# Local attention's window masks added by VectorE instead of by identity products on TensorE

## The reference

```
x  = L0_attn_x
xn = layernorm(x)
s  = xn + sum over 8 heads of  causal(relu(Q K^T)) / 512 @ V
g  = silu(ffn(xn))          # local attention + routed attention, averaged
out = x + s * g
```

```
q, k, v = split(layernorm(xn) @ w_qkv.T)            # 16 heads, DIM_HEAD 64
q, k = rope(q), rope(k)
bk = concat(previous window, own window)            # 128 keys per query
allow = (kpos >= 0) & (kpos <= qpos) & (qpos - kpos <= 64)
sim  = where(allow, q @ bk^T * 64**-0.5, -1e30)
attn = softmax(sim);  out = (attn @ bv) @ w_lo.T
```

## Time and profile before

| | |
|---|---|
| median of 3 runs (lowest, highest) | 808.0 us (806.57, 808.08) |
| the profiled execution: device time, span of its trace | 807.63 us, 805.8 us |
| mean granted TensorE clock | 0.995 |
| busy over the span: PE, DVE, ACT, POOL | 761.4 us (94%), 462.0 us (57%), 428.6 us (53%), 231.6 us (29%) |
| the 28 units of stage B that have a `b_rope` | 204.0 us |
| the last four units of stage B | 24.3 us |
| two mask products in each of 32 units | 64 weight loads of 98 ns, matmuls of 379 ns |

### The profile page before, as it was taken

How to read it: one execution, slowest core, us unless ns; L and a number is a source line. 1 busy time by engine, 2 the same in 40 slices (tenths; PEclk the granted TensorE clock), 3 DMA queues, 4 the chain that set the end, 5 groups by cost and what they waited for, 6 DMA issues and landing times.

```text
span 805.8 us, 17860 instructions
## 1 busy us (share of the span) xinstructions
PE 761.4 (94%) x6210; PEld 594.6 (74%) x6245; DVE 462.0 (57%) x1024; ACT 428.6 (53%) x1574; POOL 231.6 (29%) x373
## 2 busy tenths in 40 slices
PE   3799999999999899999999999899999999999996
PEld 3578888878876565666666667778878788797875
DVE  6422333356645887777777754665564655656454
ACT  2252444432223656766676674566574756656472
POOL 1330000000003796554455531432222323122301
PEclk9999999999999999999999999999999999999999
DMA  8600000000001323333322320000000000000001
GB/s 243 265 1 2 0 0 0 0 0 0 0 1 46 88 64 79 75 77 74 77 72 72 80 55 1 1 1 1 0 0 0 2 1 1 1 0 0 0 1 52
DMA packets 22542, 28.85 MB, mean 36 GB/s; under 512 B 6224, under 2 KB 12880, under 8 KB 21840
## 3 DMA queue, kind: packets, MB, share of 16 engines
q1 hardware_dynamic: 22480, 28.04, 12.7%
HBM read 10.19 MB, written 1.05 MB: 14 GB/s over the span
## 4 chain that ended last, share of the span: by engine, by line
PE 81%; DVE 7%; ACT 6%; issue 3%; SPq 2%; POOL 1%; DVEq 1%; DMA 0%; POOLq 0%; ACTq 0%
PE ps L706 8%; PE ps L694 8%; PE ps L963 6%; PE ps L1023 6%; PE ps L1006 6%; PE ps L755 5%; PE ps L990 5%; PE ps L681 4%; PE ps L947 4%; PE ps L675 3%; PE ps L849 3%; PE ps L861 3%; PE ps L875 3%; PE ps L825 3%; ACT stage L1251 3%
## 5 line engine op out<-in xcount | busy, mean ns | idle before, releaser
L528 POOL TENSOR_TENSOR early<-stage 128x512 f32<-128x512 f32 x64 | 81.6, 1296 | 80.1 <-DVE stage L1573 68.8
L1311 ACT ACTIVATE early<-ps,nmC 128x128 f32<-128x128 f32 (+1 forms) x224 | 78.0, 368 | 45.4 <-DVE dnC L1670 45.1
L1251 ACT ACTIVATE stage<-ps,nmB 128x128 f32<-128x128 f32 x256 | 90.3, 391 | 10.4 <-DVE nmB L1607 10.3
L706 PE MATMUL ps<-stage 128*128 128x128 f32 (+2 forms) x448 | 86.0, 320 | 1.9 <-DVE stage L1502 1.8
L694 PE MATMUL ps<-stage,early 128*128 128x128 f32 (+2 forms) x448 | 86.4, 321 | 0.0
L694 PEld LDWEIGHTS ps<-stage,early 128*128 128x128 f32 x448 | 65.2, 191 | 24.5 <-issue 15.5
L706 PEld LDWEIGHTS ps<-stage 128*128 128x128 f32 x448 | 65.3, 191 | 12.8 <-issue 2.6
L1497 DVE COPY stage<-ps 128x512 f32<-128x512 f32 x32 | 22.1, 692 | 86.6 <-PE ps L681 86.6
L1258 ACT ACTIVATE stage<-ps 128x512 f32<-128x512 f32 x64 | 34.9, 594 | 66.2 <-PE ps L861 66.2
L578 POOL TENSOR_SCALAR stage<-iota,kvcol 128x128 f32<-128x128 f32 x112 | 65.6, 601 | 6.7 <-issue 6.7
L1665 DVE TENSOR_REDUCE nmC<-ps 128x4 f32<-128x512 f32 (+1 forms) x56 | 36.5, 652 | 51.6 <-PE ps L990 51.3
(11 more groups left out here) (194 smaller groups left out, 1574.5 us busy)
## 6 DMA issues: line engine op xcount, KB each, us to landing
early<-early SPq DMA_DIRECT2D x256, 64.0 KB, 2.0
x<-in_x SPq DMA_DIRECT2D x4, 256.0 KB, 3.7
stage<-in_cq SPq DMA_DIRECT2D x1, 1024.0 KB, 5.7
stage<-in_ck SPq DMA_DIRECT2D x1, 1024.0 KB, 7.7
stage<-in_cv SPq DMA_DIRECT2D x1, 1024.0 KB, 9.7
stage<-in_co SPq DMA_DIRECT2D x1, 1024.0 KB, 12.9
early<-in_wqk SPq DMA_DIRECT2D x1, 1024.0 KB, 14.9
out<-stage SPq DMA_DIRECT2D x4, 256.0 KB, 2.3
```

The lines of the kernel that those rows point to most:

```text
L528: pool.tensor_tensor(to, a, b, (ALU.subtract, ALU.add)[f]).then_inc(rot_in, 1)
L706: t = pe.matmul(ps[:, b, q0:q1], vN[:, b % 2, m, :], simA[:, b % 2, s, at:at + q1 - q0], start=False, stop=False, skip_group_check=True)
L1251: t = act.activation(pB[:, u % 2, at, :], ps[:, 4 + h, i * P:(i + 1) * P], ACT.Exp, bias=nmB[:, u % 2, at:at + 1], accum_out=rsB[:, u % 2, ...
L1311: act.activation(pC[:, k, hg, 0:n], ps[:, 5 + k, hg * P:hg * P + n], ACT.Exp, bias=nmC[:, k, hg:hg + 1], accum_out=rsC[:, k, hg:hg + 1])
```

## The change

The mask is no longer put into PSUM. The score products write their banks directly (`start=True`). VectorE adds the fp32 mask `windowf` to each bank as it writes the sum to `pB` in SBUF (`b_mask`, one instruction of 128x512 for each head), drains, and takes the two maxima from `pB`. ScalarE takes the exponentials from `pB` to `pB` in place. TensorE's next scores wait for `masked` (both masks of the unit before added) and not for `exp_in`. The wait for the transposes two units back (`pT_out`), which guards `pB`, moves from ScalarE's exponentials to VectorE's first mask. The bf16 mask and its cast on GpSimd go.

```diff
@@ -491,7 +491,7 @@
             pool.memset(zerob[:], 0.0)
-            pool.tensor_copy(windowb[:], windowf[:]).then_inc(s_bf, 1)
+            pool.drain().then_inc(s_bf, 1)
...
@@ -829,9 +829,7 @@
             def b_scores(u):
 
                 if u > 0:
-                    pe.wait_ge(exp_in, 2 * u)
-                for h in range(2):
-                    pe.matmul(bank(4 + h), identb[:], windowb[:], start=True, stop=True)
+                    pe.wait_ge(masked, 2 * u)
...
                         t = pe.matmul(to.rearrange("p (c t) -> p c t", t=W), qT[rows, W * w:W * (w + 1)], keys,
-                                      start=False, stop=True, skip_group_check=True)
+                                      start=True, stop=True)
...
             def b_exp(u, h):
                 act.wait_ge(max_in, 2 * u + h + 1)
-                if h == 0 and u >= 2:
-                    act.wait_ge(pT_out, 2 * (u - 1))
                 for i in range(BLK):
                     at = BLK * h + i
-                    t = act.activation(pB[:, u % 2, at, :], ps[:, 4 + h, i * P:(i + 1) * P], ACT.Exp,
+                    t = act.activation(pB[:, u % 2, at, :], pB[:, u % 2, at, :], ACT.Exp,
                                        bias=nmB[:, u % 2, at:at + 1], accum_out=rsB[:, u % 2, at:at + 1])
...
+            def b_mask(u, h):
+
+                at = slice(BLK * h, BLK * (h + 1))
+                if h == 0 and u >= 2:
+                    dve.wait_ge(pT_out, 2 * (u - 1))
+                dve.wait_ge(sim_out[h], 2 * (u + 1))
+                dve.tensor_tensor(pB[:, u % 2, at], ps[:, 4 + h].rearrange("p (i n) -> p i n", n=P),
+                                  windowf[:].rearrange("p (i n) -> p i n", n=P), ALU.add).then_inc(masked, 1)
+
             def b_max(u):
+                b_mask(u, 0)
+                b_mask(u, 1)
+                dve.drain()
                 for h in range(2):
-                    dve.wait_ge(sim_out[h], 2 * (u + 1))
-                    dve.tensor_reduce(nmB[:, u % 2, BLK * h:BLK * (h + 1)], ps[:, 4 + h].rearrange("p (i n) -> p i n", n=P),
-                                      AX.X, ALU.max, negate=True).then_inc(max_in, 1)
+                    at = slice(BLK * h, BLK * (h + 1))
+                    dve.tensor_reduce(nmB[:, u % 2, at], pB[:, u % 2, at], AX.X, ALU.max, negate=True).then_inc(max_in, 1)
```

More of the change, by code:

```diff
@@ L126, in build @@
         windowf = sb("windowf", [P, BLK * P])
-        windowb = sb("windowb", [P, BLK * P], BF16)
         rmask = sb("rmask", [P, CTX])
@@ L323, in build @@
         vS_in = sem("vS_in")
+        masked = sem("masked")
         max_in = sem("max_in")
```

## The result

The changed kernel takes 847.47 us, the median of four runs (843.93 to 848.23), against 807.86 us for the kernel before beside it: a ratio of 1.0479, 95% interval 1.0459 to 1.0499, 4.8% slower. The forecast was 838, with a range to 849. The profiled execution took 843.93 us for a span of 842.1, 36.3 us more than the span before (805.8). It is the fastest of the four, and the other three took 847.3 to 848.2 us.

A forecast was written before the change was run, and what follows sets the result against it. VectorE and ScalarE's loop was to bound every unit: 6.78 + 1.37 + 0.16 = 8.31 us. Rotation units +28.7, unit 28 +1.5, last three -0.2 sum to +30.0, so 838 us, range 828 to 849.

The forecast's parts named there:

- The loop: VectorE and ScalarE: maximum, exponentials, second `b_norm`, rotation come round in 6.78 us, hidden by TensorE's 7.24; to become 8.31.
- VectorE's own round: VectorE in the steady part: 7.24 less the 0.33 us wait for TensorE's projection, 6.91 us a unit.
- The two sums and the drain: VectorE ahead of the maxima: two sums 1.30 us plus drain 0.07, first maximum 1.37 us later.
- Maxima from SBUF: VectorE's maxima reading SBUF instead of PSUM: equal within a few ns, nothing taken.
- The exponentials from SBUF: ScalarE, eight exponentials on the path reading SBUF: 0.16 us a unit taken, between nothing and 0.27.
- The early units: Units of 8.17 us delayed by GpSimd's sum meeting `b_norm`: they no longer meet, so 8.31 us too.
- Unit 28 and the tail: Behind the rotation units: remainder of unit 28 +1.5 us; last three units 19.5 us against 19.71, -0.2.
- my own range: Whole time if the forecast holds: 829 to 846 us, 84 in 100.
- the edges of two rivals: Whole time: range widened to 828 to 849 us for the edge of the clock rival and the GpSimd collision.
- TensorE as the bound: Rival: TensorE stays the bound, stage B's 19 intervals of 7.24 us fall 0.43 each, 800 us; 4 in 100.
- the collision with GpSimd: Rival: VectorE's sums and maxima delayed by GpSimd, up to 1.1 us a unit in 32 units, 873 us; 5 in 100.
- The clock rival: Rival: TensorE's clock falls as it waits about 1.5 us in every unit, +16 us, 854 us; 5 in 100.

The follow-up runs named there:

- no_masks: Kernel before without its mask products on TensorE and without mask sums, the masks left out of the result; 796.21 us, ratio 0.9855, period 6.77 us.
- two_ahead: Kernel before plus two unused VectorE maxima of 128x512 a unit, put ahead of the real maxima; 830.57 us, ratio 1.0276, period 7.97 us.
- two_behind: Kernel before plus two unused VectorE maxima of 128x512 a unit, put behind the real maxima; 809.45 us, ratio 1.0021, period 7.24 us.
- exp_from_psum: Changed kernel with exponentials reading unmasked scores in PSUM and the scores waiting for `exp_in` again; 836.67 us, ratio 1.0364, period 8.15 us.
- masks_ahead: Changed kernel with the next unit's mask sums beside this unit's exponentials and its scores issued one unit earlier; 811.41 us, ratio 1.0041, period 7.06 us.
- masks_ahead_late: Same as masks_ahead, but TensorE issues the scores behind the mix of the unit before; 814.21 us, ratio 1.0082, periods 7.08 and 7.25 us.
- after_again: Changed kernel unaltered, run again to see where its executions differ; 846.92 us, ratio 1.0480, period 8.44 us.
- filler: Changed kernel plus six unused bf16 products of 128x512 a unit on TensorE, ahead of the transposes; 847.83 us, ratio 1.0486, period 8.45 us.

## Why the prediction was right, point by point

**The loop.** Right, and shown. The floor of 6.78 us under TensorE's 7.24 is what no_masks runs at, with no TensorE line in the chain; what is put ahead of the maxima goes into the period in full (two_ahead), and behind them it doesn't (two_behind). 6.78 + 1.37 = 8.15 is exp_from_psum. One reading was wrong, though nothing in the sum used it: I took VectorE's own round as 6.91 us and explained the 6.78 of the first units by a path that the steady units have too. Most of the difference is that an instruction that waits for nothing starts 0.08 us before the end of the one ahead, and the rotation behind a wait of 0.33 us doesn't. Without that wait the steady round is 6.77 (no_masks).

**The two sums and the drain.** 1.37 us forecast, 1.37 measured. Maxima from SBUF: nothing, measured 681 against 682 ns.

**The exponentials from SBUF: the term that was mis-sized.** I took 0.16 us a unit between 0 and 0.27; it is 0.29, above my upper end. The row that I had (tanh against copy, 34 ns) is of another function, and I halved it on the thought that the next instruction's start might hide the latency. It doesn't: 43 ns of pitch each. The Trainium skill, page "VectorE: DVE Perf Modes", section on the TRN2 errata, has this for ScalarE (224 against 172 cycles at 1.2 GHz, which makes 43 ns), and the trace agrees with it. The estimate of 0.35 us a unit from that page counted eight; the 0.29 measured fits seven distances between starts, 7 x 0.043 = 0.30, with the eighth exponential lasting as long as before. 28 x 0.13 = 3.6 of the 3.9 us by which the 28 units exceed the forecast of +28.7. The other 0.3 are units 3 to 5, 8.54 us each, in which the second product of `b_norm` takes 0.79 instead of 0.69 us beside GpSimd's comparisons (L547).

**The early units.** Right. The 8.17 us intervals went to 8.43 to 8.55, without a product of 1.80 us. masks_ahead and masks_ahead_late, which moved the masks elsewhere, have products of 1.67 and 1.68 again.

**Unit 28 and the tail.** Unit 28: +1.6 (6.26 us against 4.64), forecast +1.5. The last three: 20.63 us against a forecast of 19.5. 0.4 are their exponentials; the rest lies at a fall of the clock, which I had only as a rival. TensorE and ScalarE of the changed kernel behind unit 28:

```profile
506.94 1.83 PE L859 MATMUL ps<-ident,stage 128*128 128x128 f32 x8 [3.28 <-DVE stage L1622]
507.94 0.60 ACT L1254 ACTIVATE stage<-ps 128x512 f32<-128x512 f32 x1 [1.06 <-PE ps L859]
508.56 1.91 PE L884 MATMUL ps<-stage,early 128*128 128x512 f32 x2
```

After 3.28 us of idle the eight transposes take 1.83 us instead of 1.09 and the two products 1.91 instead of 1.02, at a granted clock of 0.50 from 508 to 510 us (0.68 from 508 to 512). ScalarE copies their results ahead of its exponentials, so the next reciprocal waits 1.50 and not 1.12 us, and the scores behind come 0.45 us late.

**Behind stage B.** I had nothing there. From the end of unit 31 to the fourth copy of stage C it is 20.42 us (547.95 - 527.53) against 18.77 (511.45 - 492.68), +1.65, with this clock:

```profile
532.00:536.00 4.00, 4.00 (x15) 3.60 (x15) 0.00 (x0) 0.64 (x1) 0.00 (x0) 0.50 0.00 0
```

0.50 is the 1.2 GHz level. The 12 us behind unit 31 have a granted clock of 0.72 here (528 to 540) and had 0.86 before (494 to 506, with the 0.50 of the earlier trace rows inside). All of the +1.65 lies ahead of the second copy, which starts 12.04 us behind unit 31 (539.57) and did so 10.40 us behind it before (503.08). So the sum of the profiled execution: -0.3 (stage B's start) + 32.6 + 1.6 + 0.9 + 1.65, less 0.2 behind, is the 36.3 measured, against +30.0 forecast. The last 3.5 us, from 843.9 to the median, are executions like after_again. In all the time is 9.5 us above the forecast: about 4.2 from the exponentials (32 x 0.13). Most of the rest lies where the clock is low and in executions that differ. That it is the clock's cost is read from the place, and no run shows it apart. The measured 847.47 is above the 846 that ended my own range. It came within the 849 because I had widened the range for the edges of two rivals, and neither of them came true in the rotation units: that much was luck.

**The rivals.** TensorE as the bound fell with no_masks and the period; the collision with GpSimd with 680 and 681 ns. The clock rival was wrong where I placed it: in the steady units, with waits of 1.56 us, the granted clock is 1.00. A fall did come where TensorE had waited 3.28 us; but filler had one behind 1.90 us, so the length of the wait doesn't explain it by itself.

## What to carry to other kernels

Find the loop behind the busy engine before moving work to an engine with idle time: take the round of the chain in a stretch where the busy engine waits, and see whether the idle time lies before or behind the place where the work must go. Half a microsecond of slack under TensorE was all there was here, and the 1.45 us of VectorE's idle time could only be used by pulling the masks a unit ahead. A saving in the steady period has then to be checked against the first and last units, where both attempts lost it again, and against what lies ahead of the first unit and behind the last.

## What the runs showed of the hardware

- ScalarE's 128x128 exponential with a sum costs 43 ns more from SBUF than from PSUM in its pitch (0.387 against 0.344 us), while the durations shown for it differ by 11 ns (388 against 377). VectorE's 128x512 maximum costs the same from both.
- A VectorE sum with one operand in PSUM, and a maximum read from SBUF, run at 680 and 681 ns beside GpSimd's 2.51 us sum; the product of two SBUF operands took 1.68 us beside the same sum.
- Two executions of one kernel differed by 3 us at equal steady periods. About half of it lay between stage B and the start of stage C, where the granted clock averaged 0.57 in one and 0.72 in the other over the same 12 us (528 to 540).
- Six unused products in front of a wait cut it from 3.28 to 1.90 us, and the granted clock from 508 to 510 us was 0.51 against 0.50 without them.
